# Values products in four pieces of 128 queries instead of two of 256, between the scores products of a key tile

## What is computed

```
x = _layernorm(x + _L0_attn_ref(x, ...))              # RWKV time mix and channel mix
x = _layernorm(x + _L0_xattn_ref(x, ctx_1024, mask, ...))   # queries x, keys/values ctx, masked
x = _layernorm(x + _L0_ffn_ref(x, ...))
x = _layernorm(x + _L1_attn_ref(x, ...))              # RG-LRU block
x = _layernorm(x + _L1_xattn_ref(ctx_1024, x, ...))   # queries x, keys/values ctx
x = _layernorm(x + _L1_ffn_ref(x, ...))               # 8 experts, top 2
```

```
scores = einsum('bhsd,bhed->bhse', q, k) * att_scale
attn = softmax(scores); out = einsum('bhse,bhed->bhsd', attn, v)
```

## Time and profile before

| | |
|---|---|
| median of 3 runs | 2074.94 us (2074.53 to 2077.2) |
| the profiled execution | 2071.99 us, of which the span from first to last instruction is 2070.2 us |
| granted TensorE clock over the span | 0.932 of 2.4 GHz |
| busy share of the span | PE 86%, PEld 44%, DVE 53%, ACT 47%, POOL 14% |
| window attention | about 340 to 560 us of the span |
| wide attention | about 1040 to 1650 us |

### The profile page before, as it was taken

The page is one execution under the profiler, slowest core; times in us unless marked ns, Lnnn a source line. Parts: engine busy times, 40 slices in busy tenths (PEclk is TensorE's granted clock), DMA queues, the critical chain, the costliest instruction groups (busy, mean ns, idle before and its releaser), DMA issues. The chain is left out here.

```text
span 2070.2 us, 45934 instructions
## 1 busy us (share of the span) xinstructions
PE 1782.9 (86%) x16832; PEld 919.8 (44%) x16833; DVE 1103.8 (53%) x1492; ACT 962.8 (47%) x1695; POOL 293.5 (14%) x306
## 2 busy tenths in 40 slices
PE   6979986999979968485799999999999848999992
PEld 2334432444324423132245545545555326777771
DVE  4654236788321142543788868878878061222224
ACT  3242133777621141423178868868878731222222
POOL 4226010000020020212000000000000012222220
PEclk9989997999989989897799999999999978999996
DMA  6101032110100000217100000000000090101103
GB/s 232 37 33 50 0 60 81 37 34 26 58 1 0 0 5 0 28 22 119 60 11 11 19 11 11 12 17 11 11 10 3 2 390 29 33 30 32 34 28 130
DMA packets 54381, 88.90 MB, mean 43 GB/s; under 512 B 10800, under 2 KB 46576, under 8 KB 52282
## 3 DMA queue, kind: packets, MB, share of 16 engines
q1 hardware_dynamic: 48442, 74.28, 12.6%
q0 software_dynamic: 3648, 9.97, 1.6%
q10 hardware_dynamic: 2112, 2.10, 0.3%
HBM read 65.33 MB, written 20.58 MB: 42 GB/s over the span
## 5 line engine op out<-in xcount | busy, mean ns | idle before, releaser
L1276 ACT ACTIVATE arena<-ps 128x512 f32<-128x512 f32 x1088 | 598.5, 602 | 173.4 <-PE ps L1192 139.6
L1327 DVE TENSOR_REDUCE arena<-ps 128x1 f32<-128x802 f32 (+1 forms) x512 | 494.2, 989 | 75.8 <-PE ps L1124 74.0
L523 PE MATMUL ps<-arena 128*128 (+1 forms) x832 | 381.1, 618 | 76.1 <-DVE arena L1616 23.3
L1124 PE MATMUL ps<-arena 97*32 97x400 bf16 (+2 forms) x5120 | 359.4, 357 | 50.8 <-DVE arena L1327 22.7
L1192 PE MATMUL ps<-arena 100*32 100x512 bf16 x4352 | 389.1, 386 | 8.9 <-issue 6.0
L1167 PE MATMUL ps<-arena 128*32 128x256 f32 x4352 | 333.7, 381 | 1.5 <-ACT arena L1276 0.9
L523 PEld LDWEIGHTS ps<-arena 128*128 128x128 f32 x832 | 163.3, 198 | 292.7 <-issue 292.7
L1124 PEld LDWEIGHTS ps<-arena 97*32 97x32 bf16 x5120 | 129.8, 98 | 209.9 <-DVE arena L1327 70.4
L1802 PE MATMUL ps<-arena 128*128 x608 | 194.7, 463 | 0.8 <-ACT arena L1878 0.8
L1167 PEld LDWEIGHTS ps<-arena 128*32 128x32 f32 x4352 | 135.0, 111 | 100.9 <-issue 9.0
L1192 PEld LDWEIGHTS ps<-arena 100*32 100x32 bf16 x4352 | 120.5, 98 | 131.7 <-ACT arena L1276 32.1
(11 more groups left out here) (209 smaller groups left out, 1467.0 us busy)
## 6 DMA issues: line engine op xcount, KB each, us to landing
arena<-in_experts_w SPq DMA_DIRECT2D x8, 2176.0 KB, 18.8
arena<-qparts SPq DMA_DIRECT2D x192, 64.0 KB, 2.3
qparts<-arena SPq DMA_DIRECT2D x48, 128.0 KB, 2.0
arena<-in_ctxT SPq DMA_DIRECT2D x3, 1664.0 KB, 9.4
kparts<-arena SPq DMA_DIRECT2D x24, 208.0 KB, 2.3
arena<-kparts SPq DMA_DIRECT2D x12, 416.0 KB, 14.4
arena<-rows_out SPq DMA_DIRECT2D x8, 512.0 KB, 8.8
arena<-in_w_rwkv SPq DMA_DIRECT2D x1, 2560.0 KB, 15.0
```

The lines of the kernel that those rows point to most:

```text
L523: ins = eng.matmul(out, w[:, k, m * P:(m + 1) * P], x[:, k, tok(c)], start=k == 0, stop=k == ktiles - 1)
L1124: ins = eng.matmul(slot_banks(s_static)[j:j + 32, x, 0:n_keys], Qst[0:97, ring, heads[x], q * P + j:q * P + j + 32], Kst[0:97, at_head(rin ...
L1276: eng.activation(probs[:, keys_of(u, kt) % 2, h, :], ring_bank(r), ACT.Exp, bias=0.0).then_inc(ring_read.sem, 1)
L1327: eng.tensor_reduce(MX[:, par, heads[0] * QT + q, n % 2:n % 2 + 1], got, AX.XY, ALU.max).then_inc(slot_free.sem, 1)
```

## The change

`PV_CUTS` goes from 2 to 4, so that `PVW` is 128 queries, and `plan` places the four pieces: the first ahead of scores 2, the second behind it, and the last two behind scores 3. `pv_done` is counted up by the last of the four. All else that depends on `PV_CUTS` (the loop behind the last unit at line 1236, the condition for ScalarE's copy at line 1284) follows from the constant.

```
-            PV_CUTS = 2
+            PV_CUTS = 4
             PVW = CH // PV_CUTS
...
                     yield ("scores", kt, 1)
                     if kt == AT_DEN and u > 0 and not window:
                         yield ("den",)
+                    if has_values:
+                        yield ("pv",) + values + (0,)
                     yield ("scores", kt, 2)
                     if has_values:
-                        yield ("pv",) + values + (0,)
+                        yield ("pv",) + values + (1,)
                     if mine[1] is not None:
                         yield ("item",) + mine[1]
                     yield ("scores", kt, 3)
                     if has_values:
-                        yield ("pv",) + values + (1,)
+                        yield ("pv",) + values + (2,)
+                        yield ("pv",) + values + (3,)
```

## The result

The changed kernel takes 2089.06 us (median of 4 runs, 2088.55 to 2092.02), the kernel before 2076.07 in the same comparison: a ratio of 1.0065, 95% interval 1.0048 to 1.0083, so 13.0 us slower, between 10.0 and 17.2. The forecast was 2084.7, an increase of 9.8 us, with a range from 2074 to 2098: the sign and the main mechanisms held, and the increase was sized too small.

A forecast was written before the change was run, and what follows sets the result against it. TensorE's streaming was taken to bound both attentions outside the last units. Hand-overs of 5.4 us and copy waits of 2.6 and 1.8 us made 9.8 us, on the median 2074.94 giving 2084.7 us, range 2074 to 2098.

The forecast's parts named there:

- TensorE's queue is the path: Both attentions outside the last units: TensorE's streaming sets the time; additions to its queue are paid unless a wait shrinks.
- The first rival: Attention units: VectorE's slots set the pace and take up TensorE's added time, so not slower, 2074.9 us; 14%.
- the third: Rival, scores steps: spreading the exponentials makes it faster, at most some 10 ns in 25 tiles; 4%.
- Part 1: Values rounds: four more hand-overs of 5 ns per key tile, 20 ns in 272 key tiles, 5.4 us.
- The high end: Values rounds: each waits until its own weight load is over, 117 ns a round, 59 ns per key tile, 16 us.
- the second rival: Values rounds: loads cannot hide, so rounds last 142 ns; 64 us more, far slower, 2143 us; 7%.
- Part 2: Key tile's order: first piece ahead of the third scores step, which comes 219 ns later without starving ScalarE; at nought.
- Part 3: Key tile 1: first piece waits longer for ScalarE's values bank copy; 2.6 us wide, 1.8 us window.
- The sum within units: Both attentions: hand-overs 5.4 us plus copy waits 2.6 and 1.8 us, 9.8 us in all.
- instructions at nought: Doubled steps: two more register-computed waits per key tile run ahead of the array; at nought, without that cover 17 us.
- two begin behind the loop's return: Wide attention: two of 16 units start where the copy is long done, so they pay no longer copy wait.
- some 7: Test in the next profile: the wide attention as a whole grows by some 7 us; if not, VectorE took it up.

The follow-up runs named there:

- e5: The kernel before with the loop over chunks written out; 2061.54 us, 0.9931 of the kernel before.
- e6: The changed kernel with the loop over chunks written out; 2068.55 us, 0.9971 of the kernel before.
- e2: The kernel before with four values pieces of 128, two where each of the old ones stood, order of steps kept; 2084.52 us, 1.0033 of the kernel before.
- e1: The kernel before with its two values pieces of 256 kept, the first moved ahead of scores 2; 2084.5 us, 1.0036 of the kernel before.
- e3: The changed kernel with the first piece of key tile 1 alone put back behind scores 2; 2085.26 us, 1.0031 of the kernel before.
- e11: The changed kernel timed once more, nothing changed, beside the shifted kernels; 2090.17 us, 1.0065 of the kernel before.
- e10: The changed kernel with 20 tiny matmuls (40 instructions) ahead of everything on TensorE; 2090.88 us, 1.0073 of the kernel before.
- e4: The changed kernel with eight values pieces of 64 queries in place of its four; 2173.37 us, 1.0451 of the kernel before.
- e9: The changed kernel with 40 tiny matmuls (80 instructions) ahead of everything on TensorE; 2084.05 us, 1.0037 of the kernel before.

## Why the prediction was right, and where its sum was short

**TensorE's queue is the path.** Right. What was added to it was paid: in e5 and e6, where nothing else differs, the units grow by 0.24 and 0.33 to 0.39 us, and VectorE doesn't take it up. The first rival (not slower) is refuted: its weight loads still wait on the reduces, but the units are longer all the same. So is the third (faster).

**Part 1, the hand-over.** Right in kind, sized too high: 14 to 15 ns per key tile in e2 for the forecast 20, 3.8 us for 5.4. From start to start the 5 ns per round hold from 256 to 64 columns, and 8 x 112 - 4 x 219 is 20 ns; that the units grow by less was not traced further. The high end, a round that must wait until its own load is over, is refuted by 112 and 58 ns against loads of 111 ns, and the second rival (64 us, rounds of 142 ns) with it. The section "Back-to-back issue gap" of the Trainium skill's page "TensorE: Matmul & The Clock Gate", which the prediction had set against its sum, does not hold for four column tiles in float32: rounds of 128 columns come 112 ns apart, where that rule had made 132 of them.

**Part 2, S2 later by 219 ns at nought.** Right: 0.493 us per exponential in the last units, and e1 shows where the cover ends, at 439 ns.

**Part 3, the copy wait.** Right: the piece starts 0.14 us behind the copy in the row above, TensorE idles 0.29 us before it (0.2 to 0.3 forecast), and e1 and e3 give 5.2 and 4.6 us for the forecast 4.4. Window units pay 0.17 to 0.19 where 0.14 were charged.

**The sum within units.** 3.8 + 4.9 (between e1 and e3) = 8.7 us by the parts, 7.0 by the medians of e5 and e6, 8.3 by their ratios, 9.8 forecast: too high by 1 to 3 us.

**The term that failed: instructions at nought.** Of the instructions of the doubled steps the prediction weighed only two waits per key tile that are computed in a register, and put them at nought, since TensorE's sequencer "runs ahead of the array, which shows no gap at them". These waits were not even added; the kernel after has as many of the computations as the earlier trace rows:

```profile
L110 PEldq ALU_OP  x1332: 32/32/36, 358.8 to 1558.9; - x191
```

The supply of 32 more matmuls and weight loads per key tile had no term at all. In the middle of a unit it costs nothing at one instruction per 19 ns (e6 shows no stop; e11 shows two, of 0.2 and 0.4 us). It is not so behind the returns of the loop in the wide attention, where TensorE has stood still for want of instructions: there they come in blocks, and in the changed kernel the edge of a block lies 58 instructions behind the return, where TensorE runs dry again. The prediction had seen that "two begin behind the loop's return", and drew from it only that the copy is long done. The wide attention as a whole grew by 9.7 us in the profile where "some 7" was the test; the three units around the returns grew by 1.94, 0.78 and 2.07, some 3.6 us over their ordinary 0.4. With the loop, the change costs 13.0 us, without it 7.0 to 8.3: the missing term is 5 to 6 us, with an uncertainty of about 4 from the intervals. That 9.8 came as near to 13.0 as it did is in part luck: the parts within the units were sized too high, and this hid some of the missing term.

**What stays open.** Of these 5 to 6 us the profile places about 3.6 at the returns. From start to start, TensorE's stops at the two returns come to 10.4 us in this execution and 9.6 in e11's, against 6.7 in the kernel before, so the stops make up 2.9 to 3.8 us; what the lower clock behind them adds isn't separated, and the first stop alone varies from 2.7 to 4.2 us of idle time between executions. The rest is not settled. The stretch between the attentions has 1.9 us in this profile, but -0.3 in e11's. In the window attention four units grow by 0.5 to 1.4 us and two give back 0.3 and 0.6, so that the whole of it is 1.0 us longer than by 16 ordinary 0.24. The waits of TensorE's matmuls from 340 to 520 us show the place, in the changed kernel and in the kernel before:

```profile
PE ps L1195 <- DMA arena<-arena: 2.1, 3, 1.0
```

```profile
PE ps L1192 <- DMA arena<-arena: 0.7, 1, 0.7
```

The first scores of a unit wait there for the transfer of the unit's maxima (`store_max`). These waits differ from kernel to kernel (from 340 to 560 us 0.7 in the kernel before, 1.3 in e6, 4.1 in e10), and what sets them was not tried.

## What to carry to other kernels

Cutting a streamed matmul finer costs a hand-over per round (here 5 ns, whatever the size) and whatever the first, earlier piece must wait for: look for the one iteration in which it overwrites a buffer that another engine is still reading. Count instructions as well as columns: divide each stretch's time by the instructions of its busiest engine, set that against the pace at which the trace shows them arriving, and look behind every loop return for stops that wait on nothing but issue. If the code fits, write the loop out first (here it gave 14 us, more than the change took; the returns that lay under 6.6 us of other products showed no stop), and before pieces are merged, ask what the piece between two items hides.

## What the runs showed of the hardware that I had not expected

- A return of the loop in the wide attention leaves TensorE idle for 2.7 to 4.2 us, and a second time where the edge of a 256-instruction block comes shortly behind it: 58 instructions behind, 0.8 to 2.3 us from start to start; 18 behind, 2.9 and 3.2; with a shift of 80, none. In the window attention, where 6.6 us of output products stand around the return, no such stop shows. Behind the stops the granted clock can be at 0.50 for some microseconds.
- TensorE is given about one instruction per 16 ns in a straight stretch (256 per 4.1 us in e4); 19 ns per instruction, as after the change, runs without such stops in e6; in e11 two of 0.2 and 0.4 us show.
- Weight loads of 111 ns hide fully under rounds of 58 ns when four column tiles take turns.
- An edit of a few instructions far ahead can move or remove such a stop (58, 18, none). e9 and e11 differ by 6.1 us in all; the units right behind the returns account for 2.7 of it, and longer first stops take 1.2 back.
